# First transformer layer of a four-layer kernel: bias added in two narrower parts, copy and squares moved to ScalarE, all three engines reordered

## The reference

```python
B, DIM, HEADS, BLOCKS = (16, 48, 6, 6)      # 8x8 windows: N = 64 tokens, head width 8
def _block(x, shifted, ...):
    shortcut = x
    x = _ln(x, n1g, n1b).reshape(B, H, W, DIM)
    if shifted: x = jnp.roll(x, (-4, -4), (1, 2))
    qkv = (_win_part(x) @ qkvw.T + qkvb)...
    attn = einsum('bhnd,bhmd->bhnm', q * SCALE, k) + rpb[RPI].transpose(2, 0, 1)[None]
    if shifted: attn = attn + MASK           # -100 between different regions of a window
    attn = softmax(attn, -1)
    xw = einsum('bhnm,bhmd->bnhd', attn, v).reshape(-1, N, DIM) @ pw.T + pb
    x = shortcut + (roll back)(_win_rev(xw))
    h = _ln(x, n2g, n2b)
    return x + gelu(h @ f1w.T + f1b) @ f2w.T + f2b
# y = _ln(input); six blocks, every second one shifted; y = _ln(y); y + conv3x3(y); then layers 2 to 4
```

## Time and profile before

| what | us |
|---|---|
| median of 3 runs | 941.25 (938.55 to 941.67) |
| the profiled execution, its own time | 938.89 |
| its span in the trace | 937.1 |
| busy: PE / DVE / ACT / POOL | 766.1 / 799.4 / 571.8 / 240.3 |

### The profile page before, as it was taken

The page is one execution under the profiler, slowest core; times in us unless marked ns, Lnnn a source line. Parts: engine busy times, 40 slices in busy tenths (PEclk is TensorE's granted clock), DMA queues, the critical chain, the costliest instruction groups (busy, mean ns, idle before and its releaser), DMA issues.

```text
span 937.1 us, 20504 instructions
## 1 busy us (share of the span) xinstructions
PE 766.1 (82%) x7956; PEld 507.6 (54%) x7956; DVE 799.4 (85%) x2014; ACT 571.8 (61%) x854; POOL 240.3 (26%) x276
## 2 busy tenths in 40 slices
PE   2699999999999999999999977899877767433346
PEld 1477877788778778777777763375321111000113
DVE  7788999999999999999999955655359999999974
ACT  1376777787877877787777743133466766555133
POOL 6222222222222222222222221293121221212101
PEclk9699999999999999999999987879876755555677
DMA  8200000000000000002000000100003576657501
GB/s 235 70 2 2 2 2 2 2 2 2 2 1 3 2 2 2 1 2 108 3 2 1 2 1 1 50 1 1 1 1 62 115 138 127 127 106 135 101 0 34
DMA packets 11623, 34.14 MB, mean 36 GB/s; under 512 B 1879, under 2 KB 4359, under 8 KB 11271
## 3 DMA queue, kind: packets, MB, share of 16 engines
q0 software_dynamic: 5904, 21.24, 11.9%
q1 hardware_dynamic: 5623, 11.60, 4.1%
HBM read 10.81 MB, written 0.79 MB: 12 GB/s over the span
## 4 chain that ended last, share of the span: by engine, by line
PE 52%; DVE 36%; issue 5%; ACT 4%; POOL 1%; POOLq 0%; DVEq 0%; ACTq 0%
PE narrow L1523 7%; DVE prod L1006 4%; DVE prod L1014 4%; PE wide L1444 4%; PE scores_a L1504 4%; PE scores_b L1504 3%; PE last L1602 3%; DVE mx L613 3%; PE wide L1588 3%; PE narrow L1553 2%; PE last L1575 2%; PE narrow L1456 2%; DVE hst L1018 2%; DVE prod L1016 2%; PE scores_a L1493 2%
## 5 line engine op out<-in xcount | busy, mean ns | idle before, releaser
L381 POOL TENSOR_TENSOR stb<-stb,neg_half 128x4 f32<-128x4 f32 x48 | 48.5, 1009 | 331.0 <-DVE stb L678 331.0
L1132 ACT ACTIVATE d<-d 128x768 f32<-128x768 f32 x96 | 80.7, 841 | 16.7 <-DVE d L625 16.0
L1523 PEld LDWEIGHTS narrow<-v,pt 128*64 128x64 f32 x2304 | 82.0, 142 | 16.3 <-issue 16.3
L1523 PE MATMUL narrow<-v,pt 128*64 128x54 f32 x2304 | 88.3, 229 | 0.0
L1786 PE MATMUL scores_b<-xb,gates_w 128*32 128x512 bf16 x192 | 27.2, 584 | 63.9 <-DVE yo L1026 56.3
L1148 ACT ACTIVATE ga<-wide 128x512 f32<-128x512 f32 x48 | 28.7, 597 | 67.2 <-PE wide L1588 67.2
L607 DVE COPY v<-narrow 64x96 f32<-64x96 f32 x192 | 49.1, 256 | 13.7 <-PE narrow L1456 11.0
L1132 ACT ACT_TABLE_LOAD x46 | 59.0, 1283 | 0.8
L1156 ACT ACT_TABLE_LOAD x46 | 59.0, 1283 | 0.8
L1444 PE MATMUL wide<-xa,wts 113*120 113x256 f32 x192 | 56.2, 417 | 0.8 <-ACT xa L1108 0.8
L1602 PE MATMUL last<-wts,ga 128*128 128x48 f32 x384 | 56.4, 270 | 0.0
(11 more groups left out here) (355 smaller groups left out, 2210.5 us busy)
## 6 DMA issues: line engine op xcount, KB each, us to landing
gsum<-mag POOLq DMA_DIRECT2D x14, 512.0 KB, 4.6
ysum<-yo POOLq DMA_DIRECT2D x7, 768.0 KB, 5.6
ysum<-xd POOLq DMA_DIRECT2D x6, 768.0 KB, 5.8
gsum<-mag POOLq DMA_DIRECT2D x14, 256.0 KB, 4.8
wts<-in_wpack SPq DMA_DIRECT2D x6, 442.0 KB, 6.8
sed_w<-in_sed_in SPq DMA_DIRECT2D x1, 2304.0 KB, 8.1
graw<-in_gates_in SPq DMA_DIRECT2D x1, 1152.0 KB, 5.1
x_all<-in_x_tok SPq DMA_DIRECT2D x8, 96.0 KB, 3.0
```

The lines of the kernel that those rows point to most:

```text
L381: pool.tensor_tensor(st[n % 2].stb[:, 1], st[n % 2].stb[:, 0], neg_half[:, 0:TILES], ALU.pow).then_inc(rstd2, 1)
L1132: act.activation(d, d, ACT.Exp).then_inc(p_ready[u], 1)
L1523: op = pe.matmul(y_ps[64 * b:64 * b + 64, q * VO:(q + 1) * VO], t.pt[:, q, h, 64 * b:64 * b + 64], t.v[:, q, b, h * VO:(h + 1) * VO], star ...
```

## The change

1. **Shorter bias.** The low part lies in `bias_low` (64 partitions) and is spread by eight DMAs per block to `bias_l`, four row groups of 32. `bias` keeps one matmul of 128 rows per half, with `bias_hm`; a new stage `bias_lows` adds the low part with 16 bf16 matmuls of 32 rows by 64 columns. The mask leaves the bias: q and k get four more rows per group (28 instead of 24), fed by eight constant rows of `xa` that say in which region of the window a token lies, so that the scores matmuls add it. POOL's three fills and the three mask DMAs go; SP waits for each block's tables to issue the spreading DMAs, and for block 0 it does so ahead of the weights of blocks 1 to 5.
2. **To ScalarE.** `take_o`, `squares_a` and `squares_b`; the squares as ACT's Square with a scale, `squares_a` three slots ahead.
3. **New orders** in all three loops.

```diff
@@ sync: spread_low, called for block 0 ahead of the weights, for the others after all loads
+            def spread_low(b):
+                w = 192 * (1 + b % 2)
+                sp.wait_ge(tables_done, b + 1)
+                for r in range(2):
+                    for u in range(2):
+                        for h in range(2):
+                            sp.dma_start(bias_l[64 * r + 32 * u:64 * r + 32 * u + 32, T_OFF[b] + h * w:T_OFF[b] + (h + 1) * w],
+                                         bias_low[32 * h:32 * h + 32, T_OFF[b] + r * w:T_OFF[b] + (r + 1) * w]).then_inc(ld_low, 16)
@@ vector, the loop over k
-                squares_a(k)
                 normal_b(k - 5)
-                variance_a(k)
                 if k > 1:
                     normal_a(k - 1)
+                variance_a(k)
                 maxima(k - 3, 0)
+                subtract(k - 3, 0, 0)
                 subtract(k - 3, 0, 1)
-                subtract(k - 3, 0, 0)
-                maxima(k - 3, 1)
-                add_mlp(k - 6)
-                subtract(k - 3, 1, 1)
                 invert(k - 4)
                 divide(k - 4)
+                maxima(k - 3, 1)
+                subtract(k - 3, 1, 1)
                 subtract(k - 3, 1, 0)
...
-                take_o(k - 4)
-                take_k(k - 2)
                 add_proj(k - 4)
-                squares_b(k - 4)
+                add_mlp(k - 6)
                 variance_b(k - 4)
...
                 take_v(k - 3)
+                take_k(k - 2)
@@ scalar
+            def take_o(n):
+                if live(n):
+                    act.wait_ge(pe_oT, n + 1)
+                    if n >= 2:
+                        act.wait_ge(pe_proj, n - 1)
+                    act.activation(st[n % 2].oT[0:WIN], y_ps[0:WIN, 0:256], ACT.Copy).then_inc(o_ready, 1)
...
+                act.activation(st[n % 2].sqa[:, :, 0:C], x_all[:, n % CHUNKS], ACT.Square, scale=C ** -0.5).then_inc(sq1_done, 1)
...
+                    act.activation(st[n % 2].sqb[:, :, 0:C], x_all[:, n % CHUNKS], ACT.Square, scale=C ** -0.5).then_inc(sq2_done, 1)
...
                 exponential(k - 2, 0)
+                take_o(k - 3)
+                exponential(k - 2, 1)
+                squares_b(k - 3)
                 take_q(k - 1)
-                exponential(k - 2, 1)
                 take_PT(k - 2, 0)
                 take_PT(k - 2, 1)
-                gelu_b(k - 4)
                 affine_a(k)
+                for n in (k + 3,) if k else (1, 2, 3):
+                    squares_a(n)
...
                 affine_b(k - 3)
+                gelu_b(k - 4)
...
                 gelu_a(k - 3)
@@ tensor
+            def bias_lows(n):
...
+                for h in range(2):
+                    for b in range(2):
+                        for r in range(2):
+                            for u in range(2):
+                                g = 2 * r + u
+                                rows, off = slice(32 * g, 32 * g + 32), T_OFF[blk] + h * 192 * (1 + blk % 2)
+                                if shifted(n):
+                                    rhs = bias_l[rows, off:off + SC]
+                                    dst = sc_bank[u][64 * b:64 * b + 64, r, 0:SC]
...
+                                first = 32 * (h != u)
+                                pe.matmul(dst, ident2[rows, first:first + 64], rhs, start=False, stop=True, skip_group_check=True)
...
                 project_qk(k - 1)
-                values_T(k - 3)
+                proj(k - 3)
                 probs_T(k - 2, 0)
-                proj(k - 3)
+                project_v(k - 2)
                 probs_T(k - 2, 1)
                 fc1_b(k - 4)
-                project_v(k - 2)
                 bias(k - 1, 0)
+                windows_T(k)
                 bias(k - 1, 1)
-                windows_T(k)
+                bias_lows(k - 1)
+                transpose_z(k - 3)
                 scores(k - 1)
-                transpose_z(k - 3)
...
+                values(k - 2, 0)
+                fc1_a(k - 3)
+                values(k - 2, 1)
                 fc2(k - 4)
...
-                fc1_a(k - 3)
-                values(k - 2, 0)
-                values(k - 2, 1)
+                values_T(k - 2)
```

More of the change, by code:

```diff
@@ L317, in _ @@
             load_rpb(1)
[L318 to L319 removed]
+            spread_low(0)
             for b in range(1, BLOCKS):
@@ L326, in _ @@
                 sp.dma_start(dst, src).then_inc(ld_late, 16)
-            sp.wait_ge(tables_done, BLOCKS)
+            for b in range(1, BLOCKS):
+                spread_low(b)
             sp.dma_start(sed_w[:], sed_in).then_inc(ld_sed, 16)
@@ L729, in table_low @@
                 dve.wait_ge(mid_done, b + 1)
-                for u in range(1 + b % 2):
-                    low = bias_lm[0:64, L_OFF[b] + w * u:L_OFF[b] + w * (u + 1)]
-                    op = dve.tensor_tensor(low, rpb_sb[:, T_OFF[b]:T_OFF[b] + w], low, ALU.subtract)
-                op.then_inc(tables_done, 1)
+                low = bias_low[:, T_OFF[b]:T_OFF[b] + w]
+                dve.tensor_tensor(low, rpb_sb[:, T_OFF[b]:T_OFF[b] + w], low, ALU.subtract).then_inc(tables_done, 1)
             dve.wait_ge(set_ln, 15)
@@ L1443, in project_qk @@
                 for part, col in enumerate((W_Q, W_K)):
-                    op = pe.matmul(hid_bank[0:120, part, 0:256], w[0:WIN, col:col + 120], t.xa[0:WIN, :], start=True, stop=True)
+                    op = pe.matmul(hid_bank[0:124, part, 0:256], w[0:WIN + REG, col:col + 124], t.xa[0:WIN + REG, :], start=True, stop=True)
                 op.then_inc(pe_qk, 1)
@@ L1470, in bias @@
                 for r in range(2):
-                    for part in range(2):
-                        if shifted(n):
-                            off = (T_OFF[b], L_OFF[b] + 768 * u)[part] + SC * r
-                            rhs = (bias_hm, bias_lm)[part][:, off:off + SC]
-                            dst = sc_bank[u][:, r, 0:SC]
-                        else:
-                            off = (T_OFF[b], L_OFF[b])[part] + 192 * r
-                            rhs = (bias_hm, bias_lm)[part][:, off:off + 192].unsqueeze(1).to_broadcast([128, 2, 192])
-                            dst = sc_bank[u][:, r, 0:SC].rearrange("p (v c) -> p v c", v=2)
-                        pe.matmul(dst, ident2[:], rhs, start=(part == 0), stop=(part == 1))
+                    if shifted(n):
+                        rhs = bias_hm[:, T_OFF[b] + SC * r:T_OFF[b] + SC * (r + 1)]
+                        dst = sc_bank[u][:, r, 0:SC]
+                    else:
+                        rhs = bias_hm[:, T_OFF[b] + 192 * r:T_OFF[b] + 192 * (r + 1)].unsqueeze(1).to_broadcast([128, 2, 192])
+                        dst = sc_bank[u][:, r, 0:SC].rearrange("p (v c) -> p v c", v=2)
@@ new lines, in bias @@
+                    pe.matmul(dst, ident2[:], rhs, start=True, stop=True)
+            def bias_lows(n):
+                if not live(n):
+                    return
+                blk = n // CHUNKS
+                if n % CHUNKS == 0:
+                    pe.wait_ge(ld_low, 16 * 8 * (blk + 1))
+                for h in range(2):
[4 more added lines that the diff above has]
+                                rows, off = slice(32 * g, 32 * g + 32), T_OFF[blk] + h * 192 * (1 + blk % 2)
+                                if shifted(n):
+                                    rhs = bias_l[rows, off:off + SC]
+                                    dst = sc_bank[u][64 * b:64 * b + 64, r, 0:SC]
+                                else:
+                                    rhs = bias_l[rows, off:off + 192].unsqueeze(1).to_broadcast([32, 2, 192])
+                                    dst = sc_bank[u][64 * b:64 * b + 64, r, 0:SC].rearrange("p (v c) -> p v c", v=2)
+                                first = 32 * (h != u)
+                                pe.matmul(dst, ident2[rows, first:first + 64], rhs, start=False, stop=True, skip_group_check=True)
@@ L1969, in attn_mask @@
         ids[:, 4:] += 1
-    ids = ids.reshape(-1)
-    return np.where(ids[None, :] != ids[:, None], -100.0, 0.0)
+    return ids.reshape(-1)
 def bias_layout(rpb):
@@ L1997, in pack_l0 @@
             ch, one = slice(64 * u, 64 * u + C), 64 * u + C
+            for r in range(2 * (l % 2)):
+                for g in range(4):
+                    row, at = WIN + 4 * u, 64 * r + 32 * u + 24 + g
+                    w[row:row + 4, W_Q + at] = HD ** 0.5
+                    w[row + g, W_Q + at] = 0.0
+                    w[row + g, W_K + at] = -100.0
             for h in range(HEADS):
```

102 lines of the change are left out of this document (45 added, 57 removed).

## The result

| | before | changed |
|---|---|---|
| median, us | 938.97 (938.55 to 941.67, 5 runs) | 946.7 (946.05 to 947.22, 5 runs) |
| profiled execution: span | 937.1 | 944.5 |

The ratio of the times is 1.0074, with a 95% interval of 1.0039 to 1.011: slower by 0.7%, outside the 0.3% that can be told from no change. The forecast was 951, with 930 to 965 around it. In the later batches the kernel before had medians of 940.57 to 941.3, and the ratios of the experiments are to those. Its single executions there lie between 933.05 and 944.11 us, at mean granted clocks of 0.855 to 0.877, so one execution of it says little about a change of a few microseconds.

The account below looks back on a forecast made before the run. It took TensorE and VectorE both to be full in a first-layer slot. Unshifted slots +3.8, shifted +8.5, block 5 +2 and tables -5 gave +9.3 on 938.89, about 948.2; the median's 2.4 made 951 us, range 930 to 965.

Parts of the forecast that it names:

- rival 2: No change: shifted slots lose 0.3 us (5 us), unshifted none, tables give 5 us back; 941 us, chance 0.13.
- TensorE's row: TensorE's own stages in a first-layer slot: shorter bias against extra gaps, +0.1 us per slot, ends -0.3 and +0.3.
- the unshifted add: Unshifted slots: project_v waits 0.06 us for the residual add, since only probs_T a stands between it and proj.
- the low part: Bias on TensorE: sixteen small matmuls in two waves, 0.38 us plus 0.12 gap, 0.50 against 0.65 for four matmuls.
- The shifted add: Shifted slots: TensorE waits 0.43 us ahead of project_v for the residual add.
- Block 5: First layer's last block: TensorE's row 11.0 us, sign product delays second norm some 0.4; against 11.15, 8 x 0.25 = +2.
- Tables -5: Slots with table work: VectorE's new slack and one low copy fewer per odd block give back 5 of about 12 us.
- Start and drain 0: Start and drain of the first layer's pipeline cost 0 us, with 3 either way.
- Off VectorE and onto ScalarE: Per slot, oT copy and two squares move: VectorE then needs about 8.9 us, ScalarE 9.2 to 9.8.
- Rival 1: Faster: VectorE holds the slot and TensorE's gaps cost nothing; -14 us, so 927 us; chance 0.24.
- Rival 3: ScalarE's order: squares_b holds the PT copies, bias b starts late; 0.3 us more per slot, 965 us, chance 0.12.
- Rival 4: The low part's matmuls don't run side by side: 2.2 us more in 48 slots, over 1040 us, chance 0.03.

Follow-up runs that it names:

- run 2: Changed kernel without the low part's 16 small matmuls, so part of the bias is missing; 958.8 us (1 run).
- run 4: Kernel before with the shorter bias alone: old loop orders, copy and squares on VectorE; 932.2 us, ratio 0.989 to 0.995.
- run 3: Changed kernel with the second norm's scaling (zb) ahead of the k copy and without the low part's matmuls; 922.7 us (1 run).
- run 6: Changed kernel with fc1_b ahead of project_v on TensorE and add_mlp ahead of add_proj on VectorE; 958.6 us, ratio 1.017 to 1.025.
- Run 5: Changed kernel with normal_b behind take_v and take_k but ahead of the extra work on VectorE; 923.1 us, ratio 0.979 to 0.987.
- Runs 1: Changed kernel with normal_b (zb) moved ahead of the k copy on VectorE; 922.1 us, ratio 0.979 to 0.985.
- run 10: Kernel before with shorter bias and normal_b moved behind take_v, plus squares_a alone on ScalarE; 919.2 us, ratio 0.976 to 0.981.
- old_order_zb: Kernel before with the shorter bias alone, and normal_b moved behind take_v on VectorE; 929.1 us, ratio 0.986 to 0.991.
- zb_first_tables: Changed kernel with normal_b ahead of the k copy, and table_middle moved behind gelu_b on ScalarE; 925.7 us, ratio 0.982 to 0.989.

## Why the prediction was right, point by point

**The sum.** The step list gave +9.3 us on the profiled execution; it was +7.4 (937.1 to 944.5). It is right on the sign, and the nearness in size is luck. Only 3.4 us are in the first layer, where all of the +9.3 was meant to be, and that is nearer to rival 2's zero; the other 4.0 come from layers that the sum left out. Within the first layer terms that were too high (unshifted slots +3.8, shifted ones +8.5) and a drain that gave 3.7 stand against block 5, which cost more, and tables that gave back less.

**TensorE's row, +0.1 a slot, and +0.06 for the unshifted add: both 0.0.** Unshifted slots came out at 10.47, not 10.6. What the prediction called TensorE's row was right in one term, the low part. Low part, unshifted slot:

```profile
287.49 0.50 PE L1482 MATMUL scores_b<-bias_hm,ident 128*128 128x384 bf16 x2
287.92 0.34 PE L1504 MATMUL scores_a<-bias_l,ident 32*64 32x384 bf16 x1
...
288.11 0.32 PE L1504 MATMUL scores_a<-bias_l,ident 32*64 32x384 bf16 x1
...
288.38 0.44 PE L1590 MATMUL narrow<-ident,zb 128*128 128x128 f32 x2
```

The two bias matmuls start at 287.49; with 0.16 each, a gap of 0.11, then two waves of eight (288.11 - 287.92 = 0.19, and 0.16) and 0.09 from the last start of the second wave, 288.13, and its 0.16 to transpose_z. That is 0.46 with the gap ahead, where I had 0.50. But a shorter row is not worth its length: 0.4 us less was worth 0.03 in run 2, and 0.2 less nothing in run 4, where a copy out of the narrow bank took its place (xa in run 3, v in run 4). The low part was sized right and its price misread. That these copies close a loop all the way round the slot is argued from this and from run 6; no run follows it stage by stage. The Trainium skill (TensorEngine Tiling (Array Packing), Key Properties) says that a change of tiling mode drains the TensorE. The gaps at such changes, 0.11 and 0.09, neither show nor refute it: between bias and transposes, which use the same mode, it was 0.14 in the earlier trace rows.

**The shifted add, +0.43 a slot: right, measured +0.36** in plain shifted slots, with 0.40 idle ahead of project_v's weights. Run 4, without the new orders, has none of it, so it comes with them; run 6 shows that it isn't to be had back by moving fc1_b.

**Block 5, +0.25 in 8 slots = 2: too small, +4.0 in 7.** For the first four slots, 11.47 against 10.88 to 11.23, the step was near. But I let the sign product alone delay zb and left out that the final norm's work (zf, sqf, stf) comes ahead of it too; the last three slots took 12.13 to 12.40, against 11.20 to 11.82. Run 5 shows this share: with zb ahead of that work block 5 takes 75.5 us. The place could be seen in before, where transpose_z waited 8.8 us for zb in 16 slots; the prediction took up the wait for on alone and put the delay of zb at some 0.4 us.

**Tables -5: in part.** Start to slot 8 gave 3.1. Blocks 1 and 3 lost 2.3 each where 8 x 0.36 = 2.9 was due, so tables gave back 0.6 each; blocks 2 and 4 lost 0.9 and 0.8. Of each some 0.5 is no table work: their first slot, 11.00 against 10.47 and 10.48, still holds the shifted add of n = 15 or n = 31 (block 1 and 3 have seven such slots, not eight, by the q copies). In all about 2.6 instead of 5: the room that VectorE won was not usable, because table work stood ahead of zb. Runs 1 and 5 show that room: blocks of 85.5 to 86.9 us.

**Start and drain 0, with 3 either way:** the drain gave 3.7, for which no run separates a cause, and the unchanged layers took 4.0, which no step had. The start was right: the q copy of n = 3 comes at 56.07 against 55.84.

**Off VectorE and onto ScalarE: right.** The slots have 8.99 and 8.73 us of VectorE where 8.9 was forecast, and 8.96 and 9.08 of ScalarE, a little under the 9.2 to 9.8.

**Rivals.** Rival 1 (VectorE is the limit) holds for table slots and block 5 alone; run 10 shows it there. For plain slots it is out: 9.8 or 9.0 us of VectorE, 10.47 either way. Its test, TensorE's stages under 10.2, was too coarse, since in run 2 they are at 10.1 and the slot is 10.44. Rival 2 had the right size for the shifted slots and for unshifted ones and comes nearest to the first layer's +3.4; it missed block 5. Rival 3: bias b starts 0.3 us behind windows_T in shifted and unshifted slots, which the transposes and one gap fill, so nothing holds it; that price was not there. Rival 4 is out: the low part does run in two waves.

## What to carry to other kernels

When several transfers take turns in one bank, the copies out of it can set the slot although TensorE looks full. Here a shorter row of TensorE changed little, and cover moved from one copy to the next made it worse; look for two or three limits within a tenth of a microsecond before pricing one. An engine with slack helps only if the instruction others wait for stands ahead of its optional work: here the position of one 0.35 us instruction was worth 20 us of the first layer. Offload one operation at a time, first one that nobody waits for: `squares_a` alone, in the old order, did at least as well as the whole reordering (919.2 against 922.1 us, in different batches, both with the shorter bias and zb early).

## What the runs showed of the hardware

**The unchanged layers don't take a fixed time.** From the first y copy to the end they took 354.4 to 360.5 us in 13 profiles, with the same code. In the 14 us ahead of the first `x<-scores_a,y` the granted clock was 1.00 in before (and also in old_order_zb) and 0.78 in the changed kernel, with TensorE busy 13.13 us each time, for 117 and for 89 matmuls. One and the same kernel shows such a step too: zb_first_tables took 922.5 and 922.7 us at a mean granted clock of 0.892, and 925.6 to 926.2 in four executions at 0.871 and 0.872. The changed kernel's five executions lie within 1.2 us of each other, so whether its 4.0 us come with the change isn't shown. Up to 6 us of a difference between two kernels here can come from a part that neither of them changed; what sets it stays open.

**Sixteen matmuls of 32 rows by 64 columns start in two waves of eight,** the eight within 0.02 us (287.92 to 287.94), 0.19 apart, in the changed kernel: the low part's 6144 streamed columns take 0.35 us, where two full-width matmuls of 384 columns take 0.32 by the spacing of their starts.
